# Rows of C for the next batch: issued by ScalarE's DMA queue instead of SP's, in the scan stage of a Mamba and mixture-of-experts kernel

## The chip, the cores and the metric

The kernel runs on one core of a Trainium2 chip. A core has five engines that run their own instruction streams and meet at semaphores: TensorE (PE), VectorE (DVE), ScalarE (ACT), GpSimd (POOL) and SyncE (SP). SP here only issues DMA transfers; ScalarE can issue them too, on a queue of its own. The metric is the device time of one execution in microseconds, as the median of several runs.

## The reference, cut to what matters

The kernel computes a layer with a selective scan (Mamba) as its first half and a mixture of experts as its second. Only the scan matters here. For each of 4 batches, 1024 channels and 16 states:

```python
def step(state, xs):
    d_t, B_t, C_t, u_t = xs
    dA = jnp.exp(d_t[..., None] * A)
    state = state * dA + (d_t * u_t)[..., None] * B_t[:, None, :]
    y_t = jnp.einsum('ben,bn->be', state, C_t)
    return (state, y_t)
...
y = y + D[None, :, None] * u
y = y * jax.nn.silu(z)
```

C depends on the batch, the time step and the state, not on the channel. So one row of C (one batch, one state, 1024 time steps) serves all channels, and each of the four batches has 16 rows.

## The kernel before

The program has five stages in time: the inputs of the scan (`mamba_inputs`), the scan (`selective_scan`, from L887), a first shared pass with the routing, the experts, and a second shared pass. The change is in the scan stage alone.

The scan is cut into 32 tiles i (4 batches, 8 tiles of 128 channels each), and every tile into 16 units n, one for each state. A unit is numbered k = 16 i + n, so there are 512 of them, and a batch is 128 units. In unit k:

- TensorE multiplies the input by B (`multiply_b`, L1147): it takes du_taps (the product of step size and input, for one quarter r of the time steps) and the banded matrix m of the batch into PSUM. Half 0 of the matrix (m_first) serves units 0 to 7 of a tile, half 1 (m) units 8 to 15.
- ScalarE computes the decay exp(delta * A) into one of two PSUM buffers (L1078), and copies the matmul result of unit k + 3 from PSUM to SBUF as dbu, in two halves (`copy_input`, L1070).
- VectorE does the scan over 1024 time steps (L1108). In unit 1 of a tile it also multiplies the finished tile before by the gate (L1100).
- GpSimd multiplies the state h by the row of C (L1125). There are four buffers for h.
- TensorE adds the states up by transposing into psy (`add_state`, L1157), six units behind `multiply_b`. In units 6 to 9 of a tile it adds D * u (L1166), for which it needs the tile u. TensorE's instructions are in the order `multiply_b(k)`, `add_state(k - 6)`.

There is one buffer of SBUF for each of the 16 rows of C, `c[:, n]`, 4 KB in each of 128 partitions; a row is read from 4 KB of HBM and written to all partitions. GpSimd uses row n in all eight tiles of a batch. So the row of the next batch can only be loaded once GpSimd has done unit n of the last tile of the batch, and it is wanted 16 units later. The 16 rows of three batches (1, 2 and 3) are loaded in this way; those of batch 0 are loaded at the start of the stage.

The SP queue's order is written out by hand. In tile i it issues: the step sizes of tile i + 1 (L959, L960), the store of the gated tile i - 1 (L995), u of tile i (L987, which waits until the store has landed, since both use the tile aux), du_taps of tile i + 1 in four parts of four transfers (L967; part r waits for the matmuls of unit 12 + r of tile i), and the gate tile (L991). Around the end of a batch come the two halves of the matrix (L977, eight transfers each, after the matmuls of the units that used them last) and the rows of C (`load_c`, L981). The rows go out in four bursts: rows 0 to 3 behind the first matrix half, rows 4 to 9 behind the second, rows 10 and 11 behind the step sizes of the next tile, and rows 12 to 15 behind u of the first tile of the new batch. Each `load_c` waits on `s_hc`, GpSimd's count of finished units. All transfers of SP are on one queue, and an instruction of SP that waits holds up those behind it.

A semaphore for each row, `s_cl[n]`, tells GpSimd that its row has landed. GpSimd waits on it in the first tile of a batch.

Of the kernel before, what the change touches and what calls it, by code (L numbers as in the profile page):

```python
# [6 lines left out]
P = 128  # L7
B, L, DM = 4, 1024, 512
DI, NST, DR, DC = 1024, 16, 32, 4
# [5 lines left out]
ET = DI // P  # L15
# [38 lines left out]
def after(eng, sem, value):  # L54

    if isinstance(value, int):
        if value > 0:
            eng.wait_ge(sem, value)
    else:
        assert value.min_val > 0  # L60
        eng.wait_ge(sem, value)
# [825 lines left out]
def selective_scan(nc, io, dr, ident, arena, m0, duT, early):  # L887
# [4 lines left out]
    with ExitStack() as ctx:  # L892
# [8 lines left out]
        AHEAD, BEHIND = 3, 6  # L901
        GATED, SKIPPED = 1, 6
        GATED_AT = 8
        FIRST = 5
        m0, m1 = m0[:], sb("m", [P, TB * ROW], F32R)[:]
        skip = sb("skip", [P, P])
# [2 lines left out]
        c = sb("c", [P, NST, L])  # L909
# [22 lines left out]
        s_cl = [sem(f"p2_c_loaded{n}") for n in range(NST)]  # L932
# [8 lines left out]
        s_hc = sem("p2_state_times_c")  # L941
# [13 lines left out]
        def _(sp):  # L955
            def load_delta(i):

                after(sp, s_da, (i - 1) * NST)
                sp.dma_start(dl[:, i % 2, :], dr["dl"][i]).then_inc(s_ld[i % 2], 16)  # L959
                sp.dma_start(ad[:, i % 2, :], dr["a"][i % ET]).then_inc(s_ld[i % 2], 16)  # L960
# [15 lines left out]
                for dst_, src_ in matrix_blocks(f32((m0, m1)[half]).rearrange("p (t r) -> p t r", t=TB), dr, b, half):  # L976
                    sp.dma_start(dst_, src_).then_inc(s_m[half], 16)  # L977

            def load_c(b, n):
                after(sp, s_hc, (b * ET - 1) * NST + n + 1 if b else 0)  # L980
                sp.dma_start(c[:, n], dr["c"][b, n].partition_broadcast(P)).then_inc(s_cl[n], 16)  # L981

            def load_u(i):
                if i == 0:
                    sp.wait_ge(early["du_last"], 32)
                after(sp, s_gst, i * 16)
                sp.dma_start(ut, dr["u"][i]).then_inc(s_ut, 16)  # L987
# [27 lines left out]

            load_delta(0)
            for n in range(FIRST):
                load_c(0, n)
            load_u(0)
            load_m(0, 1)  # L1020
            for n in range(FIRST, NST):
                load_c(0, n)

            for i in range(NU):
                b = (i + 1) // ET
                turn = i % ET == ET - 1 and b < B
                turned = i % ET == 0 and i
                final = i == NU - 1
                if not final:
                    load_delta(i + 1)  # L1030
                if turned:
                    for n in range(10, 12):
                        load_c(b, n)
                if i:
                    store(i - 1)
                    load_u(i)
                if turned:
                    for n in range(12, NST):
                        load_c(b, n)
                if turn:  # L1040
                    load_m(b, 0)
                    for n in range(4):
                        load_c(b, n)
                for r in range(PARTS):
                    if not final:
                        load_du(i + 1, r)
                load_silu(i)
                if final:
                    first_weights()
                    first_tokens()  # L1050
                if turn:
                    load_m(b, 1)
                    for n in range(4, 10):
                        load_c(b, n)
            store(NU - 1)

        @block.scalar
        def _(act):
            act.dma_start(gate[:], io["g_x"].partition_broadcast(P)).then_inc(s_c, 16)

            def copy_input(k):

                if k >= SETS:
                    return
                g, r = k // GN, k % GN
                after(act, s_scan, (g - 1) * GN)
                for half in range(2):
                    act.wait_ge(s_mm, 2 * k + half + 1)
                    c0 = r * CP + half * CH
                    act.activation(dbu[:, g % 2].rearrange("p n (t c) -> p n t c", c=NC)[:, :, :, c0:c0 + CH],  # L1070
                                   product_bank(k)[:, half * CH:(half + 1) * CH].rearrange("p c t n -> p n t c"),
                                   ACT.Copy).then_inc(s_ev, 1)

            def unit(i, n, k):
                if n == 0:
                    act.wait_ge(s_ld[i % 2], (i // 2) * 32 + 32)
                after(act, s_scan, k - 1)
                act.activation(da[k % 2][:, :], dl[:, i % 2, :], ACT.Exp, scale=ad[:, i % 2, n:n + 1]).then_inc(s_da, 1)  # L1078
                copy_input(k + AHEAD)
                if k == GATED_AT:  # L1080
                    act.wait_ge(s_c, 16)
                    act.activation(gate[:], gate[:], ACT.Tanh).then_inc(s_gate, 1)
                if n == 2:

                    after(act, s_skip, i)
                    act.activation(skip[:], ident[:], ACT.Copy, scale=ad[:, i % 2, NST:NST + 1]).then_inc(s_sk, 1)

            for k in range(AHEAD):
                copy_input(k)
            units(unit)  # L1090
# [1239 lines left out]
```

## Time and profile before

| | |
|---|---|
| median of 3 runs | 3978.18 us |
| lowest, highest | 3975.2, 3978.39 us |
| profiled execution, its own time | 3982.52 us |
| its span, first to last instruction | 3980.7 us |
| scan stage, GpSimd's first to last product | 495 to 1726 us |
| granted TensorE clock, mean over the span | 0.975 |

The span is of the profiled execution, and 1.8 us lie around it. Times in the rows are counted from the start of the span. The turns of the batches lie around 771 to 862 us, 1080 to 1165 us and 1390 to 1475 us; between them the stage repeats one pattern of 16 units again and again. In the profile an engine's idle time is put down to what released it last.

### The profile page before, as it was taken

Reading aid. Unit: us, or ns where it says so; the run is one execution under the profiler, and the core shown is the slowest. Engines: PE = TensorE matmul, PEld = TensorE weight load, DVE = VectorE, ACT = ScalarE, POOL = GpSimd, SP = SyncE. Lnnn points to the kernel's source line nnn. Section 1 sums busy time; section 2 is a strip of 40 time slices with the busy share of each in tenths; the row PEclk is TensorE's granted clock in tenths of the full one; section 3 lists DMA queues with packets and bytes.
Section 4 is the critical chain, followed back from the end, with each engine's and each line's share of the span. In section 5 each row is a group of like instructions: output and inputs, shape, how many; then the busy total and the mean of one; then the engine's idle time right before and its main releaser. Section 6 shows DMA issues by size and latency. Waiting matters only on the chain. (4 is left out here: it accounts for less than half of the span.)

```text
span 3980.7 us, 58840 instructions
## 1 busy us (share of the span) xinstructions
PE 3674.5 (92%) x20528; PEld 3047.7 (77%) x20528; DVE 3058.8 (77%) x3680; ACT 2147.4 (54%) x2642; POOL 1931.1 (49%) x1169
## 2 busy tenths in 40 slices
PE   8898488888888888869999989999999999999998
PEld 3444388878878888858888868888888888888887
DVE  7898899999999999988888756666666666455555
ACT  3687689989989989942222234444444444200000
POOL 0233099999999999932222243333333333222221
PEclk9999599999999999989999989999999999999999
DMA  7677853563463473367777657777777777677543
GB/s 238 233 288 275 292 163 120 142 178 117 130 189 112 120 211 101 113 208 247 243 238 244 240 192 252 252 252 250 249 252 252 252 253 250 236 279 257 194 161 122
DMA packets 374393, 835.44 MB, mean 210 GB/s; under 512 B 96656, under 2 KB 155792, under 8 KB 364880
## 3 DMA queue, kind: packets, MB, share of 16 engines
q1 hardware_dynamic: 339264, 765.97, 56.8%
q0 software_dynamic: 34816, 67.24, 5.8%
q8 instruction: 102, 1.67, 0.2%
q14 instruction: 67, 0.55, 0.0%
q10 hardware_dynamic: 144, 0.00, 0.0%
HBM read 619.21 MB, written 245.27 MB: 217 GB/s over the span
## 5 line engine op out<-in xcount | busy, mean ns | idle before, releaser
L1125 POOL TENSOR_TENSOR h<-h,c 128x1024 f32<-128x1024 f32 x512 | 1205.6, 2411 | 29.0 <-DVE h L1108 25.9
L1108 DVE TENSOR_TENSOR_SCAN h<-da,dbu 128x1024 f32<-128x1024 f32 x512 | 1134.9, 2272 | 50.7 <-ACT dbu L1070 28.4
L1157 PE MATMUL psy<-ident,h 128*128 128x128 f32 x4096 | 562.2, 281 | 82.6 <-POOL h L1125 61.2
L1078 ACT ACTIVATE da<-dl,ad 128x1024 f32<-128x1024 f32 x512 | 583.5, 1140 | 101.8 <-DVE h L1108 89.9
L1906 POOL DMA_INDIRECT xg<-scratch_xn,ids x256 | 328.6, 1284 | 592.6 <-DVE xT_place L2199 511.6
L1070 ACT ACTIVATE dbu<-psb 128x512 f32<-128x512 f32 x1020 | 547.2, 588 | 35.0 <-PE psb L1147 34.1
L1157 PEld LDWEIGHTS psy<-ident,h 128*128 128x128 f32 x4096 | 444.6, 142 | 131.4 <-POOL h L1125 92.8
L2204 DVE TENSOR_TENSOR wsp<-arena,wsp 128x2048 fp32r<-128x2048 f32 x146 | 329.6, 2285 | 91.8 <-ACT wsp L2149 91.8
L1443 POOL DMA_INDIRECT scratch_tab<-tok_s,si_s x128 | 125.4, 980 | 459.4 <-DVE si_s L1822 375.7
L1147 PE MATMUL psb<-m,du_taps 128*128 128x128 f32 x2048 | 292.8, 290 | 42.4 <-ACT dbu L1070 35.8
L1147 PEld LDWEIGHTS psb<-m,du_taps 128*128 128x128 f32 x2048 | 257.6, 192 | 78.9 <-ACT dbu L1070 73.7
L1147 PE MATMUL psb<-m_first,du_taps 128*128 128x128 f32 x2032 | 286.5, 289 | 25.9 <-DMA du_taps<-scratch_duT 14.9
L1669 ACT ACTIVATE hT_s<-psH_s 128x512 fp32r<-128x512 f32 x64 | 38.2, 598 | 497.4 <-PE psH_s L1583 434.3
L1147 PEld LDWEIGHTS psb<-m_first,du_taps 128*128 128x128 f32 x2032 | 254.5, 196 | 32.8 <-DMA du_taps<-scratch_duT 17.7
L2149 ACT ACTIVATE wsp<-arena 128x2048 fp32r<-128x2048 f32 x146 | 273.2, 1910 | 6.8 <-DMA arena<-in_w 6.5
L488 PE MATMUL psX<-arena 128*128 128x512 f32 x512 | 232.0, 605 | 12.3 <-DMA arena<-in_ctxT 12.3
L488 PEld LDWEIGHTS psX<-arena 128*128 128x128 f32 x512 | 97.0, 195 | 123.0 <-issue 109.9
L288 POOL TENSOR_TENSOR rbuf<-lbuf,rbuf 128x1024 f32<-128x1024 f32 x20 | 47.3, 2366 | 294.2 <-DVE rbuf L789 271.3
L1733 DVE SCALAR_TENSOR_TENSOR ac_s<-arena,weights,ac_s 128x1024 f32<-128x1024 f32 x128 | 164.3, 1284 | 12.0 <-DVE ac_s L1733 0.2
L2154 ACT ACTIVATE ob<-psO 128x512 f32<-128x512 f32 x64 | 38.2, 598 | 249.1 <-PE psO L2066 249.1
L2064 PE MATMUL psG<-wsp,xT_place 128*128 128x512 f32 x384 | 150.5, 392 | 15.0 <-DVE xT_place L2199 15.0
L2215 DVE COPY ob<-psO 128x512 f32<-128x512 f32 x64 | 44.2, 691 | 154.8 <-PE psO L2066 154.8
(246 smaller groups left out, 8544.8 us busy)
## 6 DMA issues: line engine op xcount, KB each, us to landing
arena<-in_w SPq DMA_DIRECT2D x192, 1024.0 KB, 6.7
du_taps<-scratch_duT SPq DMA_DIRECT2D x496, 128.0 KB, 2.9
c<-scratch_c SPq DMA_DIRECT2D x64, 512.0 KB, 13.1
scratch_xT<-xT_s SPq DMA_DIRECT2D x32, 1024.0 KB
scratch_ob<-ob SPq DMA_DIRECT2D x64, 512.0 KB, 2.6
xT_place<-scratch_xT SPq DMA_DIRECT2D x32, 1024.0 KB, 4.9
scratch_duT<-duT SPq DMA_DIRECT2D x52, 512.0 KB, 4.1
xz<-in_x SPq DMA_DIRECT2D x32, 512.0 KB, 5.5
```

The costliest lines, as they stand in the source:

```text
L488: mm = pe.matmul(psX[q % 2][:, hb * HB:(hb + 1) * HB], w_in[:, k, et * P:(et + 1) * P], ctxT[:, b % 2, k, hb * HB:(hb + 1) * HB], start=(k ...
L1070: act.activation(dbu[:, g % 2].rearrange("p n (t c) -> p n t c", c=NC)[:, :, :, c0:c0 + CH], product_bank(k)[:, half * CH:(half + 1) * CH] ...
L1078: act.activation(da[k % 2][:, :], dl[:, i % 2, :], ACT.Exp, scale=ad[:, i % 2, n:n + 1]).then_inc(s_da, 1)
L1108: dve.tensor_tensor_scan(h[:, k % HR, :], da[k % 2][:, :], dbu[:, (k // GN) % 2, k % GN, :], 0.0, ALU.mult, ALU.add).then_inc(s_scan, 1)
L1125: pool.tensor_tensor(h[:, k % HR, :], h[:, k % HR, :], c[:, n, :], ALU.mult).then_inc(s_hc, 1)
L1147: mm = pe.matmul(product_bank(k)[:, j], duT[:, r * CP + j, :], m[g // 2][:, :, r * CP + j, g % 2 * GN:(g % 2 + 1) * GN], start=True, stop= ...
L1157: mm = pe.matmul(psy[:, t, :], h[:, k % HR, t * P:(t + 1) * P], ident[:], is_transpose=True, start=(n == 0 and t % 4 == 0), stop=(n == NST ...
L1733: dve.scalar_tensor_tensor(out=ac[:, par, :], in0=y[:, par, k, :], scalar=weights[:, bass.ds(t * TOPK + k, 1)], in1=ac[:, par, :], op0=ALU ...
L1906: return pool.indirect_dma_start(xg[:, t, g * HQ:(g + 1) * HQ], None, dr["xn"].rearrange("n (q h) -> (n q) h", q=NQ), bass.IndirectOffsetO ...
L2064: pe.matmul(dst, l[0], r[0], start=(k == 0), stop=False)
L2149: act.activation(wsp[slot][:, 0, halves[half]], raw[:, c, halves[half]], ACT.Copy).then_inc(s_whi, 1)
L2204: dve.tensor_tensor(wsp[slot][:, 1, halves[half]], raw[:, c, halves[half]], f32(wsp[slot][:, 0, halves[half]]), ALU.subtract).then_inc(s_w ...
```

## The change

SP no longer issues rows of C after the first batch: `load_c` is left for batch 0 alone. ScalarE gets a function `next_c`, called in every unit k after `copy_input(k + 3)` with `used = k - 5`. If unit `used` lies in the last tile of a batch that is not the last one, ScalarE waits until GpSimd has finished it and then issues the load of its row for the next batch. So 16 rows go out in 16 units in a row, from unit 117 to unit 132 counted from the start of the batch that ends. `after(sp, ...)` in the old code and `act.wait_ge` in the new one wait for the same count of `s_hc`. Nothing else moves.

```diff
+        USED = 5
...
-            def load_c(b, n):
-                after(sp, s_hc, (b * ET - 1) * NST + n + 1 if b else 0)
-                sp.dma_start(c[:, n], dr["c"][b, n].partition_broadcast(P)).then_inc(s_cl[n], 16)
+            def load_c(n):
+                sp.dma_start(c[:, n], dr["c"][0, n].partition_broadcast(P)).then_inc(s_cl[n], 16)
...
             for i in range(NU):
                 b = (i + 1) // ET
                 turn = i % ET == ET - 1 and b < B
-                turned = i % ET == 0 and i
                 final = i == NU - 1
                 if not final:
                     load_delta(i + 1)
-                if turned:
-                    for n in range(10, 12):
-                        load_c(b, n)
                 if i:
                     store(i - 1)
                     load_u(i)
-                if turned:
-                    for n in range(12, NST):
-                        load_c(b, n)
                 if turn:
                     load_m(b, 0)
-                    for n in range(4):
-                        load_c(b, n)
...
                 if turn:
                     load_m(b, 1)
-                    for n in range(4, 10):
-                        load_c(b, n)
...
+            def next_c(used):
+
+                b = used // (ET * NST) + 1
+                if used >= 0 and used // NST % ET == ET - 1 and b < B:
+                    n = used % NST
+                    act.wait_ge(s_hc, used + 1)
+                    act.dma_start(c[:, n], dr["c"][b, n].partition_broadcast(P)).then_inc(s_cl[n], 16)
+
             def unit(i, n, k):
...
                 copy_input(k + AHEAD)
+                next_c(k - USED)
```

## Rows read from the trace of the kernel before

**Rows 1.** Costliest groups of the page: busy us, mean ns, idle before, releaser.
```profile
L1125 POOL TENSOR_TENSOR h<-h,c 128x1024 f32<-128x1024 f32 x512 | 1205.6, 2411 | 29.0 <-DVE h L1108 25.9
L1108 DVE TENSOR_TENSOR_SCAN h<-da,dbu 128x1024 f32<-128x1024 f32 x512 | 1134.9, 2272 | 50.7 <-ACT dbu L1070 28.4
```

**Rows 2.** GpSimd's waits around the three turns: us in total, times, longest.
```profile
POOL h L1125 <- DVE h L1108: 7.4, 6, 2.5
...
POOL h L1125 <- DVE h L1108: 4.9, 5, 3.0
...
POOL h L1125 <- DVE h L1108: 4.9, 5, 2.9
```

**Rows 3.** GpSimd's timeline, three turns: start, us, instructions, idle before in brackets.
```profile
833.55 4.69 POOL L1125 TENSOR_TENSOR h<-h,c 128x1024 f32<-128x1024 f32 x2 [2.50 <-DVE h L1108]
840.60 4.94 POOL L1125 TENSOR_TENSOR h<-h,c 128x1024 f32<-128x1024 f32 x2 [2.36 <-DVE h L1108]
...
1147.54 2.39 POOL L1125 TENSOR_TENSOR h<-h,c 128x1024 f32<-128x1024 f32 x1 [2.96 <-DVE h L1108]
...
1451.14 14.22 POOL L1125 TENSOR_TENSOR h<-h,c 128x1024 f32<-128x1024 f32 x6 [2.88 <-DVE h L1108]
```

**Rows 4.** TensorE's timeline, first turn and (last row) the third.
```profile
791.00 1.12 PE L1147 MATMUL psb<-m_first,du_taps 128*128 128x128 f32 x8 [1.78 <-DMA du_taps<-scratch_duT]
...
822.74 0.68 PE L1166 MATMUL psy<-skip,aux 128*128 128x128 f32 x4 [2.19 <-DMA aux<-scratch_u]
...
834.42 1.88 PE L1147 MATMUL psb<-m_first,du_taps 128*128 128x128 f32 x8 [2.79 <-DMA du_taps<-scratch_duT]
...
1438.75 1.20 PE L1166 MATMUL psy<-skip,aux 128*128 128x128 f32 x4 [1.22 <-DMA aux<-scratch_u]
```

**Rows 5.** SP's issues in the first turn.
```profile
771.62 3.67 SPq L977 DMA_DIRECT2D m_first<-scratch_bT  x8
...
805.27 0.39 SPq L995 DMA_DIRECT2D scratch_gated<-aux  x1
819.14 0.32 SPq L987 DMA_DIRECT2D aux<-scratch_u  x1
819.50 2.21 SPq L981 DMA_DIRECT2D c<-scratch_c  x4
821.76 11.85 SPq L967 DMA_DIRECT2D du_taps<-scratch_duT  x16
```

**Rows 6.** The store and u in the middle of a batch.
```profile
653.17 0.39 SPq L995 DMA_DIRECT2D scratch_gated<-aux  x1
656.42 0.32 SPq L987 DMA_DIRECT2D aux<-scratch_u  x1
```

**Rows 7.** Stretches: engines' busy us, granted clock, DMA share, GB/s last.
```profile
776.00:780.00 4.00, 3.87 (x31) 3.32 (x31) 3.89 (x3) 3.95 (x7) 4.00 (x2) 1.00 1.08 152
788.00:796.00 8.00, 5.77 (x49) 5.10 (x46) 7.20 (x4) 5.89 (x9) 8.00 (x4) 1.00 1.03 234
810.00:815.00 5.00, 4.61 (x39) 4.12 (x38) 5.00 (x3) 4.75 (x7) 5.00 (x3) 1.00 1.03 398
...
1439.40:1442.80 3.40, 3.40 (x18) 3.40 (x18) 2.92 (x2) 1.81 (x3) 3.40 (x2) 0.50 1.00 393
```

**Rows 8.** Issues of C rows (ns min/median/max), ScalarE's one DMA, its timeline mid-batch.
```profile
L981 SPq DMA_DIRECT2D c<-scratch_c x64: 338/432/2390, 485.3 to 1436.4; - x64
...
484.10 0.39 ACTq L1059 DMA_DIRECT2D gate<-in_g_x  x1
...
646.50 1.14 ACT L1078 ACTIVATE da<-dl,ad 128x1024 f32<-128x1024 f32 x1
647.57 1.09 ACT L1070 ACTIVATE dbu<-psb 128x512 f32<-128x512 f32 x2
```

**Rows 9.** DMA queues in the expert stage, 2361.2 to 2362.4: packets, MB, share.
```profile
q1 hardware_dynamic: 182, 0.36, 77.3%
q0 software_dynamic: 45, 0.13, 27.1%
```

More of the change, by code:

```diff
@@ L1017, in _ @@
             for n in range(FIRST):
-                load_c(0, n)
+                load_c(n)
             load_u(0)
@@ L1021, in _ @@
             for n in range(FIRST, NST):
-                load_c(0, n)
+                load_c(n)
             for i in range(NU):
```

## The prediction

> **What bounds the kernel now.** The change touches one stage, so I read the page for the engine that sets the pace there, then GpSimd's waits, then its gaps, then what stands behind each gap. GpSimd multiplies one 128x1024 tile by a row of C in every unit, 512 times, back to back; VectorE's scan is almost as full [rows 1]. One unit costs GpSimd 4.69 / 2 to 14.22 / 6, so 2.35 to 2.37 us [rows 3]. It idles in any amount only where a batch ends: 7.4, 4.9 and 4.9 us around the three turns [rows 2]. That is 17.2 us, or 0.43% of the run, and the most that a better placing of the C rows can give. Four long gaps hold 2.50 + 2.36 + 2.96 + 2.88 = 10.7 us of it [rows 3].
>
> TensorE's waits say what stands behind them. In the first turn it waits 1.78 us for du_taps of unit 8, then 2.19 us for u, then 2.79 us for du_taps of unit 9 [rows 4]; the two late waits come just before GpSimd's two long gaps. SP's queue shows why. The first du_taps of unit 9 is issued at 821.76, behind u (819.14) and four C rows (819.50), and u itself had to wait for the store of 805.27: 13.9 us from store to u [rows 5], against 3.25 us in the middle of a batch [rows 6]. In between the store lay behind eight C rows. A late operand costs TensorE more than the wait. In the third turn it waited 1.22 us for u [rows 4]; right behind that the granted clock was 0.50, the 1.2 GHz level, for 3.4 us [rows 7], and GpSimd's 2.88 us gap followed.
>
> **The change part by part.** It takes 48 issues (16 rows, three turns) out of SP's program and puts them in ScalarE's, each after the two copies of a unit: row n goes out in unit 117 + n of the batch that ends (112 + n + 5). That is from about 773 us in the first turn to about 809 us, one per 2.36 us, where SP issued them from 775 to 822 in bursts of 4, 6, 2 and 4. Bytes and shapes stay.
>
> *The wait on s_hc.* Unit k waits for the product of unit k - 5. ScalarE has by then copied input k + 3, whose matmuls TensorE does after the transposes of unit k - 4, and those need the product of k - 4. So the wait is always met already: I take 0.
>
> *The issue itself.* SP needs 0.43 us for a row (0.34 to 2.39) and ScalarE's only DMA took 0.39 us [rows 8]. ScalarE's own work is 1.07 us to the next start and 1.09 us for the pair of copies, 2.16 us in a unit of 2.36 [rows 8]. Lower bound: nothing, if its sequencer issues while the copy before is still executing. Upper bound: fully exposed, the unit takes 2.16 + 0.43 = 2.59 us, 0.23 too long, 3.7 us over 16 units; the double-buffered decay absorbs about one exponential (1.14 us), so 2.6 us a turn and 7.7 us in all. I take 0, because its instructions start before the one ahead has ended (646.50 + 1.14 is past 647.57), so the sequencer is ahead of the engine, and the cover is a pair of copies of 1.09 us. Without this cover the 7.7 us stands.
>
> *What leaves SP's queue.* The last four rows were all that stood between u and du_taps of unit 9 in the queue. A row is 0.52 MB at 398 GB/s, 1.32 us, four of them 5.3 us [rows 7]. The wait was 2.79 us. With the four gone it vanishes, and with it the slow clock behind it. I also expect the store's 512 KB to no longer stand strictly behind rows.
>
> *What it collides with.* The engines that move the data are the same. From the first matrix block (771.62 [rows 5]) to the store SP has two matrix halves at 152 GB/s (6.9 us each), du_taps at 234 GB/s (9.0 us), and the gate tile and the next delta (1.3 us each): 25.4 us [rows 7]. With twelve rows (15.8 us), the store (1.3) and the 2.0 us by which the undisturbed store's 3.25 us exceeds its transfer, u goes out at 771.6 + 44.5 = 816; the trace has 819, so the sum is right within 3 us. After the change all sixteen rows are issued before or around the store. If all are served first, the store ends 5.3 us later than now; if the store goes between them, u is on time, 2.2 us earlier than now. Both ends stay for the range. The middle is 1.6 us later; I take 2, and it passes to GpSimd one to one.
>
> The nearest sign of how two queues mix is in the expert stage: in 1.2 us with weights queued on SP, GpSimd's gather got 27.1% of the DMA engines and SP's queue 77.3% [rows 9]. So a second queue does not wait for the whole first one. The Trainium skill (DMA: Bandwidth & Descriptors, "Issuing engines are not separate DMA queues") says that DMAs of all issuing engines run on the same 16 engines and interleave, and that another issuer saves only sequencer time. That speaks against this change: by it the row traffic only moves to the front of the store, which is my second rival below.
>
> **Sum.** Recovered: the four long gaps, 10.7 us, and half of the other 6.5 us, which are small gaps from having no lead after a stall: 13.9 us. Given back: u 2 us later, three times: 6 us. Issue and wait: 0. Net 8 us (0.2%). The profiled execution took 3982.5 us, so 3974.5 us; the median of the runs is 4.3 us below it, so 3970 us.
>
> **Rivals.** *Recovery in full* (0.10). Matrix blocks move at 152 and du_taps at 234 GB/s where rows reach 398 [rows 7], so rows slipped between them might travel nearly free; then u is on time and du_taps of unit 8 too, and all 17.2 us come back: 3961 us. Against: the gap hardly closes for rows beside the small-packet store.
>
> *The stall only changes its name* (0.24). The sixteen rows and the queue before the store are all served before it: 5.3 us later for u, three times 16 us, against 14 to 17 recovered. 3977 us, no change. It decides when over 12 rows are through before the store.
>
> *Rows crowd out du_taps of unit 8 and the second matrix half* (0.14, the other side). Up to unit 127 eleven rows are issued, where SP put four in front of these taps: seven more, 9.2 us, of which TensorE's 1.78 us wait shows that no slack is left. If rows are served first, GpSimd loses some 7 us more a turn, 21 us, minus 10.7 to 13.9 recovered: slower by 8 to 10, 3987 us. The weight is low because of the mixing in [rows 9]. From two rows more than now in front of the last part it starts to cost.
>
> *ScalarE is held up* (0.10). Exposed issue costs 7.7 us, which takes the gain away. If it also has to wait for an issue of SP, 0.43 us more or so each, it is 0.66 too long a unit, 10.6 - 1.1 = 9.5 us a turn, 28 us: 3980 to 3998, say 3986. The Trainium skill (Perfetto Trace Analysis, "Per-engine timelines") says that an HWDGE transfer locks one descriptor generator for exclusive use, and that the profiled time includes this lock wait. No row here shows a ScalarE issue beside a busy SP.
>
> **How the numbers follow.** A measurement of this kernel can tell about 0.2% (8 us) from no change. Forecast 0.42, with a range of its own of 3964 to 3976: 0.27 of it beyond 8 us, 0.15 within. With full recovery (0.10) and a sliver (0.02) of the second rival faster gets 0.39. Same: 0.15 + 0.17 of the second + 0.03 of ScalarE's = 0.35. Slower: 0.14 + 0.05 + 0.07 = 0.26. The range reaches to the full recovery and to the crowding case, 3961 to 3990.
>
> **What would show it.** Right: issues of c by ScalarE of 0.4 to 0.5 us and no idle time of ScalarE put down to them; in the turns no wait for du_taps of unit 9; GpSimd's waits around a turn 2 to 4 us; u issued at 813 to 821 on the old clock. Wrong: ScalarE's issues of 1 us or more; waits of TensorE for m or for du_taps of unit 8 of 5 us or more; a wait for u above 4 us, with a clock of 0.50 behind it; rows landing after GpSimd wants them (none should: row 0 has 11 units, 26 us).

## The result: slower by 24 us

| | before | after |
|---|---|---|
| median, us | 3976.69 (4 runs) | 4000.60 (4 runs) |
| lowest, highest, us | 3974.75, 3978.39 | 3997.29, 4001.86 |
| profiled execution: own time, span, us | 3982.52, 3980.7 | 3997.29, 3995.5 |
| granted TensorE clock, mean over the span | 0.975 | 0.971 |

The ratio is 1.0058 with a 95% interval of 1.0046 to 1.0071, which is 24 us and three times what a measurement of this kernel can tell from no change. The forecast was 3970.0, the range 3961 to 3990: the time lies outside of it and on the other side. The two profiled executions lie 15 us apart, because that of before was 6 us above its median and that of the change 3 us below its own; the scan stage is compared directly below. From the start of GpSimd's first product to that of its last it takes 1250.1 us instead of 1228.4, 21.7 more.

### Where the time went

The page of the changed kernel, costliest groups, to be read against [rows 1]:

```profile
L1123 POOL TENSOR_TENSOR h<-h,c 128x1024 f32<-128x1024 f32 x512 | 1205.1, 2405 | 51.2 <-DVE h L1106 48.0
L1106 DVE TENSOR_TENSOR_SCAN h<-da,dbu 128x1024 f32<-128x1024 f32 x512 | 1134.9, 2272 | 69.5 <-ACT dbu L1059 41.2
```

The products cost the same (1205.6 before). GpSimd's waits for the scan rose from 25.9 to 48.0 us, by 22.1: that is the whole growth of the stage, and nearly the 24 us of the medians. Where they lie is seen in the changed kernel's three turns (GpSimd's waits from 757 to 857, 1070 to 1170 and 1380 to 1480 us: total, times, longest), against 7.4, 4.9 and 4.9 in [rows 2]:

```profile
POOL h L1123 <- DVE h L1106: 15.9, 7, 5.1
...
POOL h L1123 <- DVE h L1106: 12.9, 5, 5.6
...
POOL h L1123 <- DVE h L1106: 10.8, 4, 6.2
```

GpSimd's timeline of the changed kernel, first turn (start, us, instructions, idle before), says on which side of the store the losses lie:

```profile
783.18 9.26 POOL L1123 TENSOR_TENSOR h<-h,c 128x1024 f32<-128x1024 f32 x4
796.35 2.35 POOL L1123 TENSOR_TENSOR h<-h,c 128x1024 f32<-128x1024 f32 x1 [3.90 <-DVE h L1106]
800.49 2.36 POOL L1123 TENSOR_TENSOR h<-h,c 128x1024 f32<-128x1024 f32 x1 [1.79 <-DVE h L1106]
807.94 4.78 POOL L1123 TENSOR_TENSOR h<-h,c 128x1024 f32<-128x1024 f32 x2 [5.09 <-DVE h L1106]
814.53 21.28 POOL L1123 TENSOR_TENSOR h<-h,c 128x1024 f32<-128x1024 f32 x9 [1.80 <-DVE h L1106]
836.12 2.39 POOL L1123 TENSOR_TENSOR h<-h,c 128x1024 f32<-128x1024 f32 x1 [0.31 <-DVE h L1106]
841.19 14.20 POOL L1123 TENSOR_TENSOR h<-h,c 128x1024 f32<-128x1024 f32 x6 [2.69 <-DVE h L1106]
```

Four gaps of 12.6 us lie at and ahead of 814.5, two of 3.0 behind it (3.3 with one more small one). The longest gap of the second and of the third turn:

```profile
1124.47 4.78 POOL L1123 TENSOR_TENSOR h<-h,c 128x1024 f32<-128x1024 f32 x2 [5.62 <-DVE h L1106]
...
1438.28 4.74 POOL L1123 TENSOR_TENSOR h<-h,c 128x1024 f32<-128x1024 f32 x2 [6.21 <-DVE h L1106]
```

The same cut, in front of the long run of products that ends at the wait for u, gives for every turn, within the windows above:

| turn | ahead: before, after | behind: before, after |
|---|---|---|
| 1 | 1.1, 12.6 | 6.3, 3.3 |
| 2 | 0.2, 11.4 | 4.7, 1.5 |
| 3 | 1.3, 10.3 | 3.6, 0.5 |
| sum of differences | 31.7 lost | 9.3 recovered |

The forecast's net gain of 8 us was all but a little in the right column, and there the chip gave 9.3. The left column is what it had at nothing. That the right column agrees is no confirmation, as the experiment with the last four rows shows.

### What stands behind the gaps

"du_taps of unit 8" and "of unit 9" are, here as in the prediction, du_taps of the tiles 8 and 9, the first two of the new batch (16 and 17, 24 and 25 in the later turns); each comes in four parts, for the first four units of the tile. TensorE's waits for transfers in the changed kernel, first turn, to be read against [rows 4]:

```profile
790.15 1.97 PE L1145 MATMUL psb<-m_first,du_taps 128*128 128x128 f32 x8 [5.34 <-DMA du_taps<-scratch_duT]
...
794.29 1.97 PE L1145 MATMUL psb<-m_first,du_taps 128*128 128x128 f32 x8 [0.45 <-DMA du_taps<-scratch_duT]
...
798.75 1.97 PE L1145 MATMUL psb<-m_first,du_taps 128*128 128x128 f32 x8 [0.76 <-DMA du_taps<-scratch_duT]
...
802.82 1.97 PE L1145 MATMUL psb<-m_first,du_taps 128*128 128x128 f32 x8 [0.38 <-DMA du_taps<-scratch_duT]
...
816.88 1.12 PE L1145 MATMUL psb<-m,du_taps 128*128 128x128 f32 x8 [1.79 <-DMA m<-scratch_bT]
...
830.38 0.68 PE L1164 MATMUL psy<-skip,aux 128*128 128x128 f32 x4 [2.86 <-DMA aux<-scratch_u]
```

The wait of 1.78 us for du_taps of unit 8 has become 5.34, and the matmuls of the four parts start 4.14, 4.46 and 4.07 us apart, where a unit takes 2.36. The waits printed in front of them are short (0.38 to 0.76), yet they pace TensorE: with each part so late, its matmuls start when it lands. A group's wait alone understates a late stream; the distance between starts shows it. The wait for du_taps of unit 9 (2.79 in [rows 4], 3.78 in the second turn, none in the third) is gone.

The code says how late parts become GpSimd's gaps: in ScalarE's program the exponential of unit k stands behind the copy of input k + 2, and VectorE's scan of the first of four units waits for the copies of all four. So in the first turn the first two gaps follow the first two parts, and the longest gap (5.09 us there, 5.62 and 6.21 in the others) follows the last part, which holds back the first unit of the new batch.

Was it the clock? It was 0.50, the 1.2 GHz level, in a window behind the 5.34 us wait (columns as in [rows 7]), and VectorE did nothing in it:

```profile
789.00:793.00 4.00, 2.85 (x13) 2.85 (x14) 0.00 (x0) 1.45 (x3) 3.45 (x2) 0.50 1.03 281
```

The third turn of the changed kernel tells the two apart, in the same view:

```profile
1420.27 1.12 PE L1145 MATMUL psb<-m_first,du_taps 128*128 128x128 f32 x8 [2.27 <-DMA du_taps<-scratch_duT]
...
1424.42 1.12 PE L1145 MATMUL psb<-m_first,du_taps 128*128 128x128 f32 x8 [2.15 <-DMA du_taps<-scratch_duT]
...
1428.90 1.97 PE L1145 MATMUL psb<-m_first,du_taps 128*128 128x128 f32 x8 [2.09 <-DMA du_taps<-scratch_duT]
...
1433.15 1.97 PE L1145 MATMUL psb<-m_first,du_taps 128*128 128x128 f32 x8 [0.56 <-DMA du_taps<-scratch_duT]
```

Eight matmuls take 1.12 us at the fast level and 1.97 at the slow one. The starts are 4.15, 4.48 and 4.25 us apart, at the fast level as at the slow one: as long as parts are late, the transfers set the pace, and the clock only turns waiting into slower work. Behind the late parts it isn't free: the matmuls of the unit that starts at 806.17 in the first turn wait for no transfer and still take 1.95 us.

Why the parts are late is in the DMA queues. First the changed kernel from 790 to 800 us, then the kernel before from 789 to 797 us (packets, MB, share):

```profile
q10 hardware_dynamic: 438, 1.60, 57.9%
q1 hardware_dynamic: 448, 1.23, 45.7%
```

```profile
q1 hardware_dynamic: 661, 1.91, 103.9%
```

q10 is ScalarE's queue. The two queues got 438 and 448 packets, as if they were served packet by packet in turn. SP's queue moved 0.123 MB per us beside it and 0.239 without it: du_taps and the second matrix half go at half the rate for as long as ScalarE's queue has rows in it. It is the packets that are shared evenly, not the bytes. From 820 to 823 us of the changed kernel SP's queue holds the store, whose packets are of 512 B:

```profile
q10 hardware_dynamic: 295, 1.08, 87.7%
q1 hardware_dynamic: 296, 0.15, 16.5%
```

There SP's queue moves 0.05 MB per us, a seventh of what the rows get.

The late parts delay the scans, those delay VectorE's multiplication by the gate, and the store goes out the moment that has finished. SP's issues in the changed kernel, first turn, against [rows 5]:

```profile
767.32 3.94 SPq L978 DMA_DIRECT2D m_first<-scratch_bT  x8
...
812.22 0.39 SPq L995 DMA_DIRECT2D scratch_gated<-aux  x1
826.39 0.32 SPq L987 DMA_DIRECT2D aux<-scratch_u  x1
```

| three turns, us | before | after | last four rows alone |
|---|---|---|---|
| first matrix issue to store | 33.6, 34.2, 35.4 | 44.9, 45.3, 44.2 | 38.0, 34.2, 35.0 |
| store to u | 13.9, 12.5, 12.3 | 14.2, 13.0, 13.7 | 16.5, 18.5, 17.7 |

The last column is an experiment below. In the change the store leaves 10.4 us later and then takes 0.7 us longer.

ScalarE's issues themselves, in the changed kernel (ns minimum, median, maximum; first and last start), against SP's 338/432/2390 in [rows 8]:

```profile
L1069 ACTq DMA_DIRECT2D c<-scratch_c x48: 326/326/374, 767.2 to 1445.7; - x48
```

No idle time of ScalarE is put down to them, and in the changed kernel GpSimd never waits for a row.

### The profile page after: what moved, and what is told of

Same layout as the page of the kernel before. It is cut to its first block and busy times, and to the rows that moved or that the text cites. A ratio compares the mean times of both kernels' runs of the same rounds, so it can differ in the third digit from the quotient of the medians.

```text
span 3995.5 us, 58840 instructions
## 1 busy us (share of the span) xinstructions
PE 3684.4 (92%) x20528; PEld 3060.6 (77%) x20528; DVE 3059.3 (77%) x3680; ACT 2149.6 (54%) x2642; POOL 1929.0 (48%) x1169
## 5 line engine op out<-in xcount | busy, mean ns | idle before, releaser
L1155 PE MATMUL psy<-ident,h 128*128 128x128 f32 x4096 | 572.3, 284 | 80.8 <-POOL h L1123 59.2
L1155 PEld LDWEIGHTS psy<-ident,h 128*128 128x128 f32 x4096 | 453.1, 144 | 129.0 <-POOL h L1123 90.5
L1145 PE MATMUL psb<-m_first,du_taps 128*128 128x128 f32 x2032 | 295.2, 294 | 30.8 <-DMA du_taps<-scratch_duT 20.6
L1145 PEld LDWEIGHTS psb<-m_first,du_taps 128*128 128x128 f32 x2032 | 262.9, 202 | 39.3 <-DMA du_taps<-scratch_duT 25.9
L488 PE MATMUL psX<-arena 128*128 128x512 f32 x512 | 229.4, 600 | 11.9 <-DMA arena<-in_ctxT 11.9
L2062 PE MATMUL psG<-wsp,xT_place 128*128 128x512 f32 x384 | 150.3, 391 | 16.6 <-DVE xT_place L2197 16.6
L2213 DVE COPY ob<-psO 128x512 f32<-128x512 f32 x64 | 44.2, 691 | 155.3 <-PE psO L2064 155.3
```

Of the source, the lines that this page charges most:

```text
L488: mm = pe.matmul(psX[q % 2][:, hb * HB:(hb + 1) * HB], w_in[:, k, et * P:(et + 1) * P], ctxT[:, b % 2, k, hb * HB:(hb + 1) * HB], start=(k ...
L1145: mm = pe.matmul(product_bank(k)[:, j], duT[:, r * CP + j, :], m[g // 2][:, :, r * CP + j, g % 2 * GN:(g % 2 + 1) * GN], start=True, stop= ...
L1155: mm = pe.matmul(psy[:, t, :], h[:, k % HR, t * P:(t + 1) * P], ident[:], is_transpose=True, start=(n == 0 and t % 4 == 0), stop=(n == NST ...
L2062: pe.matmul(dst, l[0], r[0], start=(k == 0), stop=False)
```

## The experiments

Each ratio is against the kernel before, run on the same chip; its median there was 3974.70 to 3976.69 us. GpSimd's waits are those of the scan stage, 25.9 us before and 48.0 with the change.

| kernel | median, us | ratio, interval | GpSimd's waits |
|---|---|---|---|
| the change | 4000.60 | 1.0058, 1.0046 to 1.0071 | 48.0 |
| an eighth of the bytes | 3962.76 | 0.9963, 0.9949 to 0.9977 | 9.3 |
| rows seven units later | 3992.52 | 1.0043, 1.0026 to 1.0060 | 41.7 |
| same places, SP's queue | 3988.74 | 1.0032, 1.0019 to 1.0044 | 37.6 |
| SP's order, taps first | 3985.36 | 1.0024, 1.0012 to 1.0035 | 27.4 + 6.1 |
| last four rows alone | 3991.16 | 1.0036, 1.0022 to 1.0051 | 38.0 |
| first four rows alone | 3978.19 | 1.0007, 0.9998 to 1.0017 | 26.6 |
| du_taps of units 8 and 9 on ScalarE | 3987.11 | 1.0030, 1.0020 to 1.0041 | 37.8 |
| du_taps of unit 9 on ScalarE | 3986.95 | 1.0028, 1.0018 to 1.0038 | 34.6 |
| last four rows, 4 KB store | 3991.28 | 1.0037, 1.0026 to 1.0047 | 38.8 |
| the change, 4 KB store | 3992.59 | 1.0043, 1.0030 to 1.0055 | 39.7 |
| before, 4 KB store | 3975.30 | 1.0003, 0.9991 to 1.0014 | 21.1 |
| SP's order, bursts split | 3985.55 | 1.0027, 1.0017 to 1.0037 | 34.3 |

Six kernels came out as one of their expectations had it (small rows, one queue, the first four, and all three with the other store), and rows seven units later did within 1 us. Both units of du_taps on ScalarE fell into the range of its bad case. SP's order with the taps first, the last four rows alone, du_taps of unit 9 alone and the split bursts were 6 to 9 us above the highest value expected. All four could gain by the bytes that stand ahead of the wanted transfer, so that price was too low or not the only one.

### An eighth of the bytes: issue or traffic?

The 48 issues and waits stay; each moves a row to 16 partitions, not 128, so that the other 112 multiply by the first batch's row.

```diff
-    act.dma_start(c[:, n], dr["c"][b, n].partition_broadcast(P))...
+    act.dma_start(c[0:16, n], dr["c"][b, n].partition_broadcast(16))...
```

> The changed kernel, but each of the 48 rows that ScalarE loads goes to 16 partitions only instead of 128 (64 KB instead of 512 KB), so GpSimd multiplies 112 partitions by the row of the first batch. All waits, ScalarE's 48 issues and their places stay. Theory A (the bytes of the rows take the DMA engines from du_taps of unit 8, the matrix halves and u): with 7/8 of the bytes gone the turns lose almost nothing, TensorE's waits for du_taps at the turns fall under 1 us, GpSimd's waits in the stage fall from 48 to under 15 us, and the time is 3958 to 3966 us, below the kernel before. Theory B (ScalarE's issues or its wait on s_hc hold it up): the waits stay, the time stays above 3990 us.

GpSimd's waits in this kernel, then its issues:

```profile
POOL h L1123 <- DVE h L1106: 9.3, 11, 3.9
```

```profile
L1069 ACTq DMA_DIRECT2D c<-scratch_c x48: 308/308/373, 772.2 to 1412.2; - x48
```

13 us faster than before, with all of the change's instructions in place. They cost nothing that shows, and the loss is traffic: bytes or packets, since both are an eighth here. It also measures what the turns have to give: 25.9 - 9.3 = 16.6 us, near the 17.2 of [rows 2].

### Rows seven units later

```diff
-        USED = 5
+        USED = 12
```

> The changed kernel with USED = 12 instead of 5: ScalarE issues every row seven units (16.5 us) later, from unit 124 to unit 139, so most of du_taps of unit 8 is through first. Theory A: the 5.3 us wait for du_taps of unit 8 goes (under 2.5 us), and the conflict moves to the second matrix half, u and du_taps of unit 9, which then share with rows: the waits for m, u or du_taps of unit 9 grow to 3 to 6 us. In all better than the change, not better than before: 3980 to 3992 us. Theory B: the same number of issues, 4000 us. A theory C (the half clock behind the long first stall makes most of the loss): 3975 to 3983 us, since no stall is as long as 5 us.

TensorE in the first turn of this kernel:

```profile
826.06 1.20 PE L1164 MATMUL psy<-skip,aux 128*128 128x128 f32 x4 [6.45 <-DMA aux<-scratch_u]
```

The waits for du_taps fall from 20.6 to 10.6 us in all (longest 2.3), those for u rise from 5.8 to 17.4. The stall moves with the rows: at neither place did the second queue find room for them.

### Same places, one queue

Rows go back to SP, as near as its order allows to where ScalarE put them: rows 0 to 3 as before, one behind each part of du_taps of unit 8, 8 and 9 behind the second matrix half, ten to thirteen ahead of the store, the last two behind it and ahead of u.

```diff
                         load_du(i + 1, r)
+                    if turn:
+                        load_c(b, 4 + r)
...
-                    for n in range(4, 10):
+                    for n in range(8, 10):
...
-                    for n in range(10, 12):
+                    for n in range(10, 14):
...
                     store(i - 1)
-                    load_u(i)
                 if turned:
-                    for n in range(12, NST):
+                    for n in range(14, NST):
                         load_c(b, n)
+                if i:
+                    load_u(i)
```

> The kernel before, with SP issuing the rows at about the places in time where the change has them: rows 0 to 3 behind the first matrix half, one row behind each of the four parts of du_taps of unit 8, 8 and 9 behind the second matrix half, 10 to 13 ahead of the store and 14, 15 behind it, ahead of u. Nothing on ScalarE. If it is the bytes ahead of du_taps that count, whichever queue they are on, this is as slow as the change, 3995 to 4005 us. If it is the second queue, whose rows are served packet by packet beside SP's and so also slow the matrix half that stands ahead of du_taps, then one queue loses less: du_taps of unit 8 waits 3 to 5 us in all instead of 7, u about 4 us, du_taps of unit 9 nothing, 3982 to 3992 us.

TensorE's wait for du_taps over the scan stage of this kernel:

```profile
PE psb L1150 <- DMA du_taps<-scratch_duT: 18.6, 12, 2.8
```

13 us of the 24 come with the places alone; what is left, 11 us, lies between this kernel and the change, so it belongs to the second queue and to the order that the two kernels don't share. There is no wait for u in this one.

### SP's order, taps first

Row 0 goes behind du_taps of unit 8, rows 1 to 7 behind the second matrix half, rows 8 to 11 between the store and u, and the last four one behind each part of du_taps of unit 9.

```diff
-                if turned:
-                    for n in range(10, 12):
-                        load_c(b, n)
                 if i:
                     store(i - 1)
-                    load_u(i)
                 if turned:
-                    for n in range(12, NST):
+                    for n in range(8, 12):
                         load_c(b, n)
+                if i:
+                    load_u(i)
                 if turn:
                     load_m(b, 0)
-                    for n in range(4):
-                        load_c(b, n)
...
                         load_du(i + 1, r)
+                    if turned:
+                        load_c(b, 12 + r)
...
+                    load_c(b, 0)
                     load_m(b, 1)
-                    for n in range(4, 10):
+                    for n in range(1, 8):
```

> The kernel before with another order of SP's queue, no second queue: du_taps of unit 8 directly behind the first matrix half, row 0, the second half, rows 1 to 7; rows 8 to 11 behind the store instead of ahead of it; rows 12 to 15 one behind each part of du_taps of unit 9. Theory A says that what counts is only what stands ahead of the three wanted transfers: the wait for du_taps of unit 8 (1.8 us) goes, the store is 5.3 us earlier and u's wait (2.2 us) goes, and du_taps of unit 9 waits under 1 us. GpSimd's waits around the turns fall from 17 to 3 to 8 us: 3963 to 3971 us. If the total of bytes in a turn is the limit, the time is 3975 to 3979 us, as before. Against it: row 0 lands just when it is wanted, and rows could be late by 1 to 3 us.

GpSimd's waits in the scan stage of this kernel:

```profile
POOL h L1124 <- DVE h L1107: 27.4, 18, 3.9
...
POOL h L1124 <- DMA c<-scratch_c: 6.1, 5, 3.5
```

The wait for du_taps of unit 8 is gone, and 7.1 us for u, 7.7 for du_taps of unit 9 and 6.1 for rows that are now late stand in its place.

### The last four rows alone, and the first four alone

Only those rows go through ScalarE; SP keeps the others where they were.

```diff
+        ROWS = range(12, 16)        # the other kernel: range(4)
...
+                if used >= 0 and ... and used % NST in ROWS:
```

> The kernel before, with only rows 12 to 15 taken from SP's queue and issued by ScalarE (units 129 to 132, USED = 5); rows 0 to 11 stay where they were on SP. This is the step that the prediction summed: du_taps of unit 9 no longer has four rows ahead of it, u gets up to four rows more ahead of it or beside it. If the sum was right apart from the crowding of unit 8: the wait for du_taps of unit 9 (2.8, 3.8 us) goes, u's wait grows from 1.0-2.2 to 3-4 us, and the time is 3968 to 3974 us. If a wait for u costs as much as one for du_taps and the half clock follows it as well, it is 3975 to 3985 us.

> The kernel before, with only rows 0 to 3 issued by ScalarE (units 117 to 120), the other twelve on SP as they were. Ahead of du_taps of unit 8 there stand the same bytes as before, only on the other queue and beside the first matrix half instead of behind it. Theory 'bytes' (what counts is what has to be moved before du_taps): no change, 3973 to 3980 us, the wait for du_taps of unit 8 stays 2 us. Theory 'second queue' (rows beside the matrix half and the taps slow them more than their bytes cost): this alone costs 3 to 4 us a turn, 3984 to 3990 us.

SP's store and u in the second turn of the kernel with the last four, then TensorE's wait for u over its scan stage:

```profile
1119.23 2.86 SPq L997 DMA_DIRECT2D scratch_gated<-aux  x1
...
1137.78 0.32 SPq L989 DMA_DIRECT2D aux<-scratch_u  x1
```

```profile
PE psy L1174 <- DMA aux<-scratch_u: 19.0, 3, 7.3
```

This is the edit that the forecast's argument was about: these were the four rows between u and du_taps of unit 9. Alone they lose 16.5 us. The waits for du_taps fall as forecast, from 14.9 to 6.8 us, but those for u grow from 4.4 to 19.0. GpSimd's gaps behind the cut, where the forecast had a net gain of 8 us, grow from 14.6 to 23.5. From store to u it takes 16.5, 18.5 and 17.7 us, 4.7 more than before on average, close to the 5.3 us that four rows take by [rows 7]: so they go ahead of the store's last packets, or among them. In the second and third turn du_taps of unit 8 are waited for by 0.7 and 2.3 us, where it was none and 2.6 before; in the first by 3.8, where it was 2.4, and the store is late there too (38.0 us). The first four alone, hardly moved in time, change nothing that the runs can tell: the second queue costs by what it overtakes, not by being used.

### Taps on ScalarE instead of rows

The turned-round split: rows stay on SP, and ScalarE issues du_taps, of the units named "8" and "9" in the first kernel and of "9" alone in the second.

```diff
-                    if not final:
+                    if not final and not at_turn(i):
                         load_du(i + 1, r)
...
                 copy_input(k + AHEAD)
+                if at_turn(i) and 0 <= n + AHEAD - (NST - PARTS) < PARTS:
+                    load_du(i + 1, n + AHEAD - (NST - PARTS))
```

> The inverse of the change: all rows stay on SP as in the kernel before, and ScalarE issues du_taps of the two units at each turn (4 transfers in each of 4 units, twice a turn), the transfers that TensorE is about to want. Theory A (a second queue gets its share of the DMA engines packet by packet, whatever is queued on the first): du_taps of unit 9 lands about 4 to 5 us after its issue instead of 12, the waits for du_taps at the turns (15 us in the stage, with those of the start) fall under 3 us, and the time is 3963 to 3970 us. Against it: 32 issues a turn of 0.33 us, four in a unit, 1.3 us beside 2.16 us of copies and exponentials; if they are not hidden ScalarE's unit takes 3.5 us and the time is 3985 to 4000 us.

> As the kernel before, all rows on SP, but ScalarE issues only du_taps of unit 9 of each turn (16 transfers); du_taps of unit 8 goes back to SP, where the run with both units on ScalarE showed it slowed by sharing with the matrix half and rows 4 to 9 (waits up to 5.5 us), while the wait for unit 9 was gone. Theory A: no wait for du_taps of unit 9, the rest as before: GpSimd's gaps of 2.4 to 3 us behind it go, 3 to 8 us saved, 3967 to 3973 us. If ScalarE's four issues in a unit (idle times of 0.5 to 0.9 us in that run) cost what they save, 3973 to 3978 us.

TensorE in the first turn of the first kernel and ScalarE's waits for its own issues over its scan stage, then ScalarE in the first turn of the second:

```profile
804.93 1.97 PE L1161 MATMUL psb<-m_first,du_taps 128*128 128x128 f32 x8 [5.49 <-DMA du_taps<-scratch_duT]
```

```profile
ACT da L1090 <- issue: 16.5, 21, 2.0
```

```profile
826.43 2.40 ACTq L1083 DMA_DIRECT2D du_taps<-scratch_duT  x4
828.88 1.14 ACT L1090 ACTIVATE da<-dl,ad 128x1024 f32<-128x1024 f32 x1 [1.85 <-issue]
```

With both, nothing waits for u or for du_taps of unit 9 any more, but the last part for unit 8 comes 5.49 us late beside the rows of SP, and ScalarE's exponentials wait 16.5 us for the issues in front of them. With one, four issues in a row occupy ScalarE's sequencer for 2.40 us and its next exponential starts 1.85 us late: 7.2 us of such waits in all. The waits for du_taps of unit 9 don't even go with it: 2.7, 2.3 and 3.2 us in the three turns, 2.8, 3.8 and none before.

### The store in packets of 4096 B

The store writes 128x1024 values; as it stands, in 1024 packets of 512 B. Here it writes its rows whole, so that the gated values land in other places of the buffer.

```diff
-  dr["gated"][i // ET].rearrange("(t p) (e c) -> e p t c", p=P, c=P)[i % ET], aux[:]
+  dr["gated"][i // ET].rearrange("(e p) h -> e p h", p=P)[i % ET], ut
```

> The kernel with only rows 12 to 15 on ScalarE's queue (3991.2 us, waits for u of 5.1 to 7.3 us), but every store of a gated tile writes a block of whole token rows (4096 bytes a packet) instead of a block of columns (512 bytes a packet), so the gated values stand in the wrong places; bytes are the same. Theory 'packets': the store has 64 small packets on each DMA engine and each waits for one 4096-byte packet of a row on the other queue, so with 8 packets the store lands 5 to 9 us earlier, the waits for u fall under 2.5 us and the time is 3970 to 3979 us. Theory 'bytes' (u is late since four rows more are moved before it): no change, 3986 to 3992 us.

> The changed kernel with the same edit of the stores (blocks of whole token rows, 4096-byte packets; gated values in the wrong places). Theory 'packets': only the part of the loss that comes from u goes: the waits for u (2.9, 1.3, 1.7 us) fall under 1 us, while du_taps of unit 8 and the second matrix half still wait; 3986 to 3996 us. Theory 'bytes': 3996 to 4002 us.

> The control: the kernel before with the same edit of the stores (4096-byte packets; gated values in the wrong places). With one queue the store's packets have nothing to alternate with, it only moves 512 KB in 1.3 us instead of 1.7 us: u is 0.4 to 1 us earlier, 3970 to 3977 us.

TensorE's waits over the scan stage of the change with this store:

```profile
PE psb L1145 <- DMA du_taps<-scratch_duT: 17.2, 12, 4.4
...
PE psb L1145 <- DMA m<-scratch_bT: 6.0, 3, 2.5
```

Against its own kernel before the change is 17 us slower with it, not 24, though the two intervals overlap. Store to u takes 11.9, 10.4 and 9.9 us, 2.9 less on average, no wait for u is left, and GpSimd's waits fall by 8.3. The kernel before gains nothing in time (1.0003), but its waits fall too, by 4.8, so not all of the 8.3 can be counted. The kernel with the last four rows gains nothing (19.0, 19.1 and 17.4 us from store to u). So small packets beside large ones probably cost some in the change, where the rows are spread out, which isn't clear of the noise; they are no part of the loss where four rows arrive together.

### SP's order, bursts split

Rows 2 and 3 go behind du_taps of unit 8, rows 14 and 15 behind the second part of du_taps of unit 9.

```diff
-                    for n in range(12, NST):
+                    for n in range(12, 14):
...
-                    for n in range(4):
+                    for n in range(2):
...
+                    if turned and r == 1:
+                        for n in range(14, NST):
+                            load_c(b, n)
+                if turn:
+                    for n in range(2, 4):
+                        load_c(b, n)
```

> One queue, the kernel before with two bursts of rows split around du_taps: rows 2 and 3 go out behind du_taps of unit 8 instead of ahead of it, rows 14 and 15 behind the second part of du_taps of unit 9. What the runs so far say is that a transfer is late by what is moved before it, 1.3 us a row. Two rows fewer are 2.6 us: the waits of 1.8 to 2.6 us for unit 8 go, those of 2.8 and 3.8 us for unit 9 shrink to 0.2 and 1.2 us, u stays where it is. GpSimd's waits in the stage fall from 26 to 16 to 21 us, and the time is 3966 to 3972 us. Against it: rows 2, 3, 14 and 15 land 9 and 4 us later and could be missed by GpSimd, and the third and fourth parts of du_taps of unit 9 stand behind two rows; then 3974 to 3979 us.

TensorE in the first turn of this kernel:

```profile
820.83 1.20 PE L1172 MATMUL psy<-skip,aux 128*128 128x128 f32 x4 [4.11 <-DMA aux<-scratch_u]
...
838.54 1.97 PE L1153 MATMUL psb<-m_first,du_taps 128*128 128x128 f32 x8 [4.03 <-DMA du_taps<-scratch_duT]
```

No wait for du_taps of unit 8 is left. What two rows gave back there is lost at u (2.19 before, 4.11 here) and at du_taps of unit 9 (2.79 and 4.03).

### What the experiments have in common

Windows of 62 us around the first turn (columns as in [rows 7]): the kernel before, the change, the kernel with an eighth of the bytes, and the one with the taps first:

```profile
773.50:835.50 62.00, 51.26 (x400) 46.92 (x399) 56.23 (x26) 50.15 (x71) 58.38 (x25) 0.96 0.97 267
```

```profile
769.00:831.00 62.00, 49.31 (x338) 46.04 (x337) 47.89 (x23) 44.34 (x62) 49.32 (x22) 0.81 0.98 250
```

```profile
769.00:831.00 62.00, 56.08 (x451) 50.95 (x451) 60.28 (x29) 56.96 (x81) 61.73 (x28) 1.00 0.77 167
```

```profile
771.50:833.50 62.00, 53.35 (x415) 50.53 (x415) 54.65 (x26) 51.37 (x74) 56.52 (x25) 0.92 0.85 246
```

The DMA engines are 97% busy before and 98% after, and at that share the change moves 250 GB/s, the kernel before 267; only with fewer bytes (0.77) is GpSimd busy for nearly all of the window. So in the change there was no room beside the rows. It is not true of every order that lost: the kernel with the taps first has a share of 0.85 in this window, of 0.55 from 820 to 829 us, and those with one queue and with split bursts have 0.94. In those 9 us SP issued one part of du_taps at 819.02 and the next only at 825.21: each part waits for matmuls, and the rows behind it wait with it. A hand-made order thus has two prices, who stands ahead, and how long the queue runs empty at a wait; what each took of the 9 to 13 us wasn't separated.

## Why the prediction was wrong

**The step that failed is "What it collides with".** It added up the bytes of a turn as one stream, in the order of issue, and asked only how late u would be; for du_taps of unit 8 and the second matrix half the sum had nothing. These are what the rows collide with first. The wait for the first part was 5.34 us in the first turn, and the matmuls of the four parts started 4.1 to 4.5 us apart instead of 2.36. All that is late ahead of the store cost GpSimd 11.5, 11.2 and 9.0 us in the three turns, 31.7 in all. With the 9.3 us recovered, the net is 22.4 in the turns, against 22.1 for the whole stage and 24 in the runs.

**The mechanism was the third rival**, *Rows crowd out du_taps of unit 8 and the second matrix half*, at the 0.14 that it was given. It named the place and the slack (none, by the 1.78 us wait of [rows 4]), and was still short in size: 7 us a turn against 10.6, and 10.7 to 13.9 us recovered against 9.3 (its own numbers give a loss of 7 to 10 us, not 8 to 10). It took the seven more rows as a block in front of the taps. On the chip they run beside them, and while they do, the taps go at half the rate; behind the taps the second matrix half is late too (a wait of 1.79 us for m in the first turn).

**[rows 9] were read the wrong way round.** They show that GpSimd's queue does not wait for what SP's has queued. The prediction took that as a reason for a low weight of the crowding. But the sum of shares in those rows is 104%: what one queue gets, the other does not, and in a full stretch the other is SP's with the operands that are due. The Trainium skill (DMA: Bandwidth & Descriptors, "Queues, rings and completion order") describes the service by each DMA engine as a rotation over the queues that have work, packet by packet. In the packets that the profile counts the trace agrees, by 438 against 448 and by 295 against 296; the page's packet can hold several descriptors, and whether it is the same unit no run here shows.

**"u 2 us later"** was off too, but not in the way that cost the time. Counted from the first matrix issue u came 11.1 us later on average; 10.4 of it is the late store, and that is the crowding again, seen from further down. The store's own landing grew by 0.7. With the last four rows alone this term stands nearly alone: 4.7 us, near its upper bound of 5.3. So it was mis-sized as well: three times 4.7 is 14 us, as much as the forecast hoped to recover, and that kernel lost 16.5.

**"Recovered" agreed by luck.** The forecast had a net gain of 8 us behind the store, and 9.3 were seen. But the edit that was to give it, alone, made the same gaps 8.9 us longer. In the change the store left 10.4 us later, behind the loss in front; no run that moves all the bytes shows the gain without that loss.

**What was right.** *The wait on s_hc* and *the issue itself* at 0: 326 ns, none of it exposed, and the kernel with small rows gains 13 us with all of them in it. *What leaves SP's queue*: no wait for du_taps of unit 9 is left. Rows are in time. *ScalarE is held up* did not occur. *Recovery in full* is near what the kernel with an eighth of the bytes reached, but for the opposite reason: not by slipping between the others, only by leaving most of their bytes out. Of its signs, one of those for "wrong" came: a wait of 5 us or more for du_taps of unit 8. GpSimd's waits around a turn were 15.9, 12.9 and 10.8 us, not 2 to 4.

**A warning that the numbers held.** [rows 7] had the DMA share at 1.00 or above in all four stretches. With that, "what leaves the queue" isn't a gain by itself: the bytes stay in the same 62 us, and the question is in front of whom.

**What stays open.** How much of the 11 us between the one-queue kernel and the change is the sharing, and how much the slightly different places, wasn't separated. That the slow clock adds little while parts are late is argued from the third turn, not tested, and what it costs behind them wasn't separated. Seven other placements lost as well, three of them with all rows and taps on SP's queue, so the order before is the best that was tried, which doesn't show it to be the best there is. No version beat it that moves all the bytes.

## What to carry to other kernels

Before a transfer goes to a second engine's queue, look at the DMA share of the stretch. Where it is near 1, the move is a change of order: the moved transfers take turns, packet by packet, with everything on the first queue. So list the operands that are due in that stretch and price each at half of the packets, the first one first; that was half the rate for du_taps here, and far less for a store in small packets. What helped in this stretch was fewer bytes; starting some of them in an emptier one was not tried.

## What the runs showed of the hardware that was not expected

- Two busy hardware queues got the same number of packets (438 and 448 in 10 us), and the first queue's rate fell from 0.239 to 0.123 MB per us. With packets of 512 B on one and rows on the other it was so too (296 and 295 in 3 us), and the bytes were 0.15 and 1.08 MB.
- The same issue of a row took 326 ns on ScalarE, 374 at most, beside a full SP queue; on SP it took up to 2390 ns. Four issues in one unit were another matter: 2.40 us for four, and 1.85 us of it exposed.
- TensorE at the slow level (1.97 us for eight matmuls) and at the fast one (1.12) advanced at the same pace, a unit in 4.1 to 4.5 us, as long as its operands came at that pace.
